# Fixing the expert of the first eight pairs of token tiles in the last mixture-of-experts layer

## The reference, cut to what matters

```python
router_logits = x_flat @ gate_w.T                    # 2048 tokens, E = 8
top_w, sel = jax.lax.top_k(router_logits, TOPK)      # TOPK = 2
top_w = jax.nn.softmax(top_w, axis=-1)
tw = jnp.zeros((n, E), dtype=x.dtype).at[tok_ids, sel].add(top_w)
g = jnp.einsum('nd,efd->enf', x_flat, gate_proj)     # F_DIM = 352
u = jnp.einsum('nd,efd->enf', x_flat, up_proj)
h = jax.nn.silu(g) * u
eo = jnp.einsum('enf,edf->end', h, down_proj)
out = jnp.einsum('end,ne->nd', eo, tw)
```

## Time and profile before

| | |
|---|---|
| median of three runs | 3435.64 us (3432.76 to 3437.16) |
| the profiled execution's own time | 3431.57 us |
| its span in the trace | 3429.8 us |
| PE busy | 3125.4 us (91% of the span) |
| DVE, ACT, POOL busy | 2102.3, 1293.4, 1478.2 us |
| end of the routing, from PE's first instruction to the experts' first | 3012.62 to 3042.85 us |

### The profile page before, as it was taken

One profiled execution on the slowest core, in us unless ns is written; L12 is line 12 of the kernel. 1 busy time (PEld: TensorE's weight loads), 2 busy tenths in 40 slices (PEclk: granted clock), 3 DMA queues, 4 the chain that ended last, 5 costly groups with the idle time before them and its releaser, 6 DMA issues. The chain is left out here.

```text
span 3429.8 us, 58056 instructions
## 1 busy us (share of the span) xinstructions
PE 3125.4 (91%) x20720; PEld 2611.0 (76%) x20720; DVE 2102.3 (61%) x3794; ACT 1293.4 (38%) x3291; POOL 1478.2 (43%) x1470
## 2 busy tenths in 40 slices
PE   7999999999969999899896999699999999969991
PEld 5887878878857777678674777488888888759991
DVE  5666566676636767621185777566667677745566
ACT  3343333333336666401222333244444444324440
POOL 4554343444422343310163222255555556545565
PEclk9999999999989999889997999799999999979996
DMA  4001016022310111149574112210101001147665
GB/s 175 16 13 57 0 36 235 0 79 104 141 48 26 48 34 62 69 164 339 173 166 123 37 40 65 98 60 25 47 12 48 11 24 38 47 172 242 238 228 159
DMA packets 137869, 317.13 MB, mean 92 GB/s; under 512 B 18425, under 2 KB 30457, under 8 KB 135538
## 3 DMA queue, kind: packets, MB, share of 16 engines
q1 hardware_dynamic: 120194, 274.61, 23.7%
q0 software_dynamic: 15360, 36.25, 4.2%
q10 hardware_dynamic: 2160, 4.21, 0.3%
HBM read 231.07 MB, written 98.04 MB: 96 GB/s over the span
## 5 line engine op out<-in xcount | busy, mean ns | idle before, releaser
L398 POOL TENSOR_TENSOR a_sq<-a_tq,a_sinq 128x256 f32<-128x256 f32 x128 | 150.5, 1195 | 357.0 <-DVE a_tq L476 355.7
L398 POOL TENSOR_TENSOR a_sk<-a_tk,a_sink 128x256 f32<-128x256 f32 x128 | 124.0, 988 | 90.0 <-DVE a_tk L476 90.0
L364 ACT COPY a_probT<-bank 128x512 f32<-128x512 f32 x64 | 37.5, 587 | 327.4 <-PE bank L715 327.4
L411 POOL TENSOR_TENSOR e_sk<-e_tk 128x512 f32<-128x512 f32 x64 | 66.5, 1039 | 203.1 <-DVE e_tk L503 203.1
L353 ACT ACTIVATE e_prob<-bank,e_nb,e_rq 128x128 f32<-128x128 f32 x256 | 114.0, 456 | 85.8 <-DVE e_nb L577 85.8
L348 ACT ACTIVATE a_sm<-a_sm,a_nmax 128x128 f32<-128x128 f32 x256 | 99.9, 392 | 121.7 <-DVE a_nmax L572 121.7
L954 ACT ACTIVATE b_prob<-bank,b_nb 128x128 f32<-128x128 f32 x512 | 139.4, 387 | 10.3 <-DVE b_nb L1152 10.3
L1048 POOL TENSOR_TENSOR d_prob<-d_prob,d_nmax 128x1024 f32<-128x1024 f32 x32 | 64.0, 1998 | 183.3 <-DVE d_nmax L1147 183.3
L2482 POOL TENSOR_TENSOR n_wu_lo<-nw_wu,n_wu_hi 128x1408 fp32r<-128x1408 f32 x23 | 74.3, 3231 | 127.2 <-DVE n_wu_hi L2526 127.2
L498 DVE TENSOR_TENSOR a_kr<-a_kr,a_sk 128x512 f32<-128x512 f32 x64 | 66.4, 1037 | 89.1 <-POOL a_sk L398 89.1
L1149 DVE TENSOR_REDUCE b_nmax<-bank 128x8 f32<-128x1024 f32 x64 | 77.7, 1215 | 63.6 <-PE bank L1293 62.8
(11 more groups left out here) (542 smaller groups left out, 10753.5 us busy)
## 6 DMA issues: line engine op xcount, KB each, us to landing
packed<-all_zero SPq DMA_DIRECT2D x32, 1024.0 KB, 8.9
cw_wg<-in_c_wg SPq DMA_DIRECT2D x32, 512.0 KB, 5.2
cw_wu<-in_c_wu SPq DMA_DIRECT2D x32, 512.0 KB, 6.1
cw_wd<-in_c_wd SPq DMA_DIRECT2D x32, 512.0 KB, 8.4
nw_wg<-in_f_wg SPq DMA_DIRECT2D x23, 704.0 KB, 5.6
nw_wu<-in_f_wu SPq DMA_DIRECT2D x23, 704.0 KB, 7.6
nw_wd<-in_f_wd SPq DMA_DIRECT2D x23, 512.0 KB
nw_xe<-packed SPq DMA_DIRECT2D x46, 256.0 KB, 2.7
```

The source lines that it names most:

```text
L364: nc.scalar.copy(probT[:], pP[:, :]).then_inc(act_pt, 1)
L398: step = nc.gpsimd.tensor_tensor(o, i, s, ALU.mult)
```

## The change

The first eight pairs now belong to experts 0 to 7 in this order, whatever the routing: pair `e` holds the first 256 rows of expert `e`. Only what an expert has beyond 256 tokens goes to the pairs from the ninth on, by the tables as before. There are still 23 pairs, and each is computed as before.

So neither the number nor the place of the first eight pairs is read from a table. SP loads the first pair's weights at the beginning of the end of the routing, waits for the sends, then loads both pairs' tokens, then the second pair's weights. The experts' first three rounds of refills (pairs 2 to 7) are written out instead of looped. Two sends move from the end of the routing into cross-attention. DVE gets more to do for the tables and for `rows`: a token's result now lies in one of two places of its expert, depending on whether its position is below 256. The wait on `tabled` falls away.

```diff
@@ wide_attention, POOL, last slot
                 if router and last:
+                    for n in (2, 3):
+                        router.send(pool, (b - 5) // 2, n)
                     pool.drain()
@@ end_of_routing
         @block.sync
         def _(sp):
-            sp.wait_ge(tabled, 2)
+            weights.load(sp, weights.number(sp, 0, 0), 0)
+            sp.wait_ge(router.sent, 16 * K * B)
             for w in range(2):
-                weights.load(sp, weights.number(sp, 0, w), w)
-                if w == 0:
-                    sp.wait_ge(router.sent, 16 * K * B)
                 weights.load_x(sp, router.packed.rearrange("(t r) d -> t r d", r=P), weights.place(sp, 0, w), w)
+            weights.load(sp, weights.number(sp, 0, 1), 1)
 
         @block.gpsimd
         def _(pool):
-            for n in (2, 3):
-                router.send(pool, LAST - 2, n)
             for p in (LAST - 1, LAST):
...
             step(vec.tensor_reduce(first[:, 1:NE + 1], summed[:], AX.X, ALU.add))
+            step(vec.tensor_scalar(first[:], first[:], float(NE), None, ALU.add))
...
-            vec.tensor_scalar(weights.expert[:], texp[:], float(NE - 1), None, ALU.min).then_inc(tabled, 1)
+            step(vec.tensor_scalar(weights.expert[:], texp[:], float(NE - 1), None, ALU.min))
...
+            step(vec.tensor_scalar(tsum[:], tsum[:], float(1 - NE), 0.0, ALU.add, ALU.max))
...
-            step(vec.scalar_tensor_tensor(out=npair[:], in0=first[:, 0:NE], scalar=float(PAIR), in1=region[:], op0=ALU.mult, op1=ALU.subtract))
-            step(vec.tensor_tensor(prod[:], hot[:], npair[:].unsqueeze(1).unsqueeze(1).to_broadcast([P, K, B, NE]), ALU.mult))
-            step(vec.tensor_reduce(pos[:].rearrange("p b k -> p k b"), prod[:], AX.X, ALU.add))
-            step(vec.tensor_tensor(rows[:], rowf[:], pos[:], ALU.add))
+            step(vec.tensor_scalar(edge[:], region[:], float(PAIR), None, ALU.add))
+            step(vec.scalar_tensor_tensor(out=low[:], in0=iota[:, 0:NE], scalar=float(PAIR), in1=region[:], op0=ALU.mult, op1=ALU.subtract))
+            step(vec.scalar_tensor_tensor(out=more[:], in0=first[:, 0:NE], scalar=float(PAIR), in1=edge[:], op0=ALU.mult, op1=ALU.subtract))
+            step(vec.tensor_tensor(more[:], more[:], low[:], ALU.subtract))
+            for each_expert, out in ((edge, pos), (low, own), (more, over)):
+                step(vec.tensor_tensor(prod[:], hot[:], each_expert[:].unsqueeze(1).unsqueeze(1).to_broadcast([P, K, B, NE]), ALU.mult))
+                step(vec.tensor_reduce(out[:].rearrange("p b k -> p k b"), prod[:], AX.X, ALU.add))
+            step(vec.tensor_tensor(pos[:], rowf[:], pos[:], ALU.is_ge))
+            step(vec.tensor_tensor(over[:], over[:], pos[:], ALU.mult))
+            step(vec.tensor_tensor(own[:], own[:], over[:], ALU.add))
+            step(vec.tensor_tensor(rows[:], rowf[:], own[:], ALU.add))
@@ RoutedWeights.place (number has the same two lines, without the factor)
+        if isinstance(i, int) and 2 * i + w < self.NE:
+            return (2 * i + w) * (REGION // P)
@@ routed_experts, SP
-            with sp.Fori(0, ROUNDS - 1) as i:
+            FIXED = weights.NE // 2 - 1
+            for i in range(FIXED):
+                for w in range(2):
+                    refill(i, w)
+            with sp.Fori(FIXED, ROUNDS - 1) as i:
```

More of the change, by code:

```diff
@@ L2093, in end_of_routing @@
         pos, prod = st.sbuf("pos", [P, B, K]), st.sbuf("prod", [P, K, B, NE])
+        low, more, edge = st.sbuf("low", [P, NE]), st.sbuf("more", [P, NE]), st.sbuf("edge", [P, NE])
+        own, over = st.sbuf("own", [P, B, K]), st.sbuf("over", [P, B, K])
         apart, expd, total = st.sbuf("apart", [P, B]), st.sbuf("expd", [P, B]), st.sbuf("total", [P, B])
@@ L2099, in end_of_routing @@
         texp, tsum = st.sbuf("texp", [P, NP]), st.sbuf("tsum", [P, NP])
-        act_e, v_c, tabled = st.sems("act_e", "v_c", "tabled")
+        act_e, v_c = st.sems("act_e", "v_c")
         block = ctx.enter_context(nc.Block())
@@ L2133, in _ @@
             each = [P, NE, NE]
-            step(vec.tensor_scalar(limit[:], iota[:, 0:NE].unsqueeze(1).to_broadcast(each), float(PAIR), None, ALU.mult))
+            step(vec.tensor_scalar(limit[:], iota[:, 0:NE].unsqueeze(1).to_broadcast(each), float(PAIR), float(PAIR), ALU.mult, ALU.add))
             step(vec.tensor_tensor(limit[:], limit[:], region[:].unsqueeze(2).to_broadcast(each), ALU.add))
@@ L2156, in _ @@
             step(vec.tensor_tensor(tsum[:], iota[:, 0:NP], tsum[:], ALU.subtract))
+            step(vec.tensor_scalar(tsum[:], tsum[:], float(1 - NE), 0.0, ALU.add, ALU.max))
             step(vec.scalar_tensor_tensor(out=tsum[:], in0=texp[:], scalar=float(REGION // PAIR), in1=tsum[:], op0=ALU.mult, op1=ALU.add))
-            vec.tensor_scalar(weights.tile[:], tsum[:], 2.0, float(NE * REGION // P - 2), ALU.mult, ALU.min).then_inc(tabled, 1)
-            step(vec.scalar_tensor_tensor(out=npair[:], in0=first[:, 0:NE], scalar=float(PAIR), in1=region[:], op0=ALU.mult, op1=ALU.subtract))
-            step(vec.tensor_tensor(prod[:], hot[:], npair[:].unsqueeze(1).unsqueeze(1).to_broadcast([P, K, B, NE]), ALU.mult))
-            step(vec.tensor_reduce(pos[:].rearrange("p b k -> p k b"), prod[:], AX.X, ALU.add))
-            step(vec.tensor_tensor(rows[:], rowf[:], pos[:], ALU.add))
+            step(vec.tensor_scalar(weights.tile[:], tsum[:], 2.0, float(NE * REGION // P - 2), ALU.mult, ALU.min))
+            step(vec.tensor_scalar(edge[:], region[:], float(PAIR), None, ALU.add))
[9 more added lines that the diff above has]
+            step(vec.tensor_tensor(rows[:], rowf[:], own[:], ALU.add))
             dve.wait_ge(act_e, 1)
@@ L2356, in number @@
     def number(self, sp, i, w):
+        if isinstance(i, int) and 2 * i + w < self.NE:
+            return 2 * i + w
         return sp.value_load(self.expert[0:1, bass.ds(2 * i + w, 1)], min_val=0, max_val=self.NE - 1)
```

## The result

| | before | after |
|---|---|---|
| median of eight runs | 3435.51 us (3426.30 to 3437.27) | 3425.18 us (3421.48 to 3427.88) |
| ratio, with its 95% interval | | 0.9973 (0.9962 to 0.9983) |
| profiled execution, own time | 3431.57 us | 3424.73 us |
| its span | 3429.8 us | 3422.9 us |

The kernel became faster by 0.27%, 5.8 to 13.1 us by the interval, 6.9 us between the two traces. The prediction was 3429.0 us, a gain of 6.6 us, with 0.52 on "no difference that can be measured". The direction was right. The 0.27% lies above the 0.2% that the prediction set as the limit of what can be told from no change, so by that limit the likelier class was the wrong one, though the interval reaches down to 0.17%.

The account below looks back on a forecast made before the run. The prediction took the gap ahead of the experts, where PE waits at a barrier for SP, as the bound. Landing 4.6 plus SP 2.2 gave 6.8, taken as 6.6: 3435.6 to 3429.0 us, range 3425.5 to 3433.0.

Parts of the forecast that it names:

- no difference that can be measured: Whole kernel: the result class for a gain below about 0.2% (6.9 us), given 0.52 against 0.43 for faster.
- The landing of the sends: End of the routing: with pair 0's weights issued early, the last send lands 4.6 us sooner; lower bound 3.5.
- SP's issues: Between landing and barrier: without three table reads SP needs 3.9 us, not 6.1; gain 2.2, bounds 1.1 to 2.7.
- a slow issue: SP's transfers after the landing: one or two slow issues among eight would cost 0.7 to 1.1 us.
- The moved sends: Cross-attention: the two sends moved there give nothing by themselves, covered by some 7.7 us of POOL's idle time.
- the refills: Experts, pairs 2 to 7: transfers without table loads may go 1.5 us earlier; counted 0, up to 0.4 gained.
- the longer tables: End of the routing: DVE's 12 more instructions take 3.8 us, hidden, as DVE ends 2.6 us ahead of SP.
- The releaser of PE's long wait: Barrier ahead of the experts: the releaser shown beside PE's 21.48 us wait is only the last engine to arrive.
- The lead of the second pair's weights: Start of the experts: pair 1's weights are issued 1.9 us before PE begins, 1.7 us less lead; hidden.
- DVE holding up the last sends: End of the routing: DVE locking out GpSimd could delay two sends by 0.2 us each, 0.4 in all; left out.
- Transfers of all engines share the DMA engines: End of the routing: four sends beside pair 0's weights land later, but have until 3030.4; sum unchanged.
- How the numbers follow: Whole kernel: parts' bounds give 3427.4 to 3432.5 us, run scatter about 2 us; range and class chances follow.

Follow-up runs that it names:

- e2: The kernel before with only the first pair's weights issued at the beginning of the end of the routing; 3432.00 us, ratio 0.9991.
- e6: The changed kernel with SP waiting for DVE's tables before the first pair's weights, so they run beside the last sends; 3435.74 us, ratio 1.0004.
- e7: The changed kernel with SP again reading both pairs' token places and the second pair's number from tables after the sends; 3430.58 us, ratio 0.9982.
- e3: The changed kernel with the two moved sends put back behind the barrier; 3428.28 us, ratio 0.9980.
- e8: The changed kernel with the refills of pairs 2 to 7 made in the loop and read from the tables; 3427.84 us, ratio 0.9980.
- e12: The changed kernel with 16 small dependent instructions added at the end of DVE's work in the end of the routing; 3421.51 us, one run.
- e9: The changed kernel with the second pair's weights issued behind the barrier, at the start of the experts; 3414.96 us, ratio 0.9969.
- e4: The changed kernel with both pairs' weights issued ahead of the wait for the sends; 3427.43 us, ratio 0.9977.
- e1: The kernel before, unchanged, measured again for the scatter; 3437.16 us, ratio 1.0005.
- e5: The changed kernel, unchanged, measured again beside the kernel before; 3429.26 us, ratio 0.9986.
- e11: As e10, with DVE working out the gate weights while it waits for PE's last counts; 3416.13 us, ratio 0.9969.
- e10: As e9, with the second pair's tokens also issued behind the barrier; 3415.66 us, ratio 0.9969.

## Why the prediction was right, and where it was not

- *The landing of the sends*, forecast 4.6 us: right. 4.3 to 4.4 by e2, 4.4 by e6. It rested on one send of four that took 7.3 us, and on which transfers stood ahead of it.
- *SP's issues*, forecast 2.2: right, 2.1 by e7. SP took 3.9 us from the landing to its end, to the tenth that was forecast. That the tenth fits has some luck in it: the terms written there add up to 3.81 and not 3.85, most issues in a row took 0.43 us, against 0.33 to 0.38 in the kernel before, and a slow issue did come, the last one: SP's last two took 1.15 us, and 0.95 to 0.97 in e3 and e8. The stretch shrank by 6.74, nearer the sum of 6.8 than the 6.6 that I took.
- *The moved sends, the refills, the longer tables*, all at 0: right, by e3, e8 and e12. DVE's end moved by 3.8 us as counted.
- *The releaser of PE's long wait*, read as the last engine at the barrier: wrong, and without effect on the sum. Line 65 is `head_start`, the first thing that DVE does behind the barrier. The step on which the sum rests, to take each engine's own last instruction, was right.
- *The lead of the second pair's weights*: 1.75 us by the prediction's own times (3034.3 and 3036.05), not 1.9; measured 1.75. No new wait appeared.
- *DVE holding up the last sends*: the eight sends' issues took 0.97 to 1.17 us beside DVE's longer run too, with one of 1.17 as before, and the last came 14.89 us after PE's first instruction (15.06 before). The prediction weighed a loss of 0.4 by the rule of the Trainium skill (SBUF — State Buffer, "SBUF: two separate sides") and left it out of the sum; no trace here shows one.
- *Transfers of all engines share the DMA engines*, the other rule weighed (the Trainium skill, DMA: Bandwidth & Descriptors, "Issuing engines are not separate DMA queues"): the traces agree. In e9, which is the changed kernel up to there, the first send behind the barrier, issued while the weights ran, landed after 3.7 us and the last four after 2.7 to 2.9. It cost the changed kernel nothing, but 0.9 us when 3.8 MB instead of 1.9 MB of weights ran ahead (e4).
- *How the numbers follow* is the step that was weak. I set the range from terms known to a tenth of a microsecond and a scatter of "about 2 us" read from three runs that lay 4.4 us apart. On one chip before's runs then lay 10.8 us apart (e1), on the next 21.3 (e5), and the medians of the same changed kernel gave 9 us once and 5 us once (e5). That e5's median (3429.26) is almost the likeliest time of 3429.0 is in part luck, since the interval of its ratio is 9 us wide; 3425.18, the first, is outside the range by 0.3. With a true gain of 6.7 us, the line of 0.2% runs through the middle of what a measurement can show, and my 0.43 against 0.52 said little more than that.

The part of the first median beyond 6.7 us was not traced run by run. That it is scatter of the clock is argued and not shown. It rests on e1 and e5, on the times at which the end of the routing begins (3013.4 to 3018.0 in e5 to e8, on one chip and with the same program up to there; 3007.7 to 3018.0 over all chips), and on the granted clock of long and short runs.

## What to carry to other kernels

When an engine waits for small transfers, look at what runs on the DMA engines beside them: a big load that nobody needs yet can cost several times its own issue. It helped to move it well ahead (e2), while putting twice as much there took back 0.9 of 2.1 us (e4). Where a barrier follows, its issues too belong behind that barrier, if nobody needs it at once (e9). Make addresses constant where a read from a table stands between a wait and a barrier; in the refills it was worth nothing that shows (e8). Read who holds a barrier from each engine's own last instruction: the releaser beside PE's wait was another one in e9 to e11, and what held PE was the barrier as before. And measure a change of some microseconds in a kernel of milliseconds by the distance between two instructions of one trace, which repeated to 0.2 us here, while the total moved by ten and more.

## What was not expected of the hardware

The version to build on is e9 (0.9969, 0.9957 to 0.9981, with the shortest edit). Its stretch is 2.1 us shorter than the changed kernel's; that its total is shorter too is not shown, since the intervals overlap and the two did not stand on one chip. e10 and e11 shorten the stretch further but their totals can't be told from it. What bounds all three is a chain: 17.8 to 17.9 us until the last send has landed, SP's issues of the tokens or DVE's last instructions (until 19.6, 19.2 and 18.7), and 1.8 us of barrier. The tokens' way back, 2.5 to 2.7 us for the first tile, ran beside it and had caught up only in e11. The scatter of the granted clock was larger than I knew: the same twelve products took 2.99 us in one trace and 5.49 us in another, by the level at which they happened to run.
